# Double-norm roots in one power, dot products in two column parts, and tail weights sent earlier, in an eight-stage graph and feed-forward kernel

## What is computed

```
# layer 0, graph part: 8 heads, then a last attention with one head
h      = z @ W2                               # 128 x 768, summed over 8 heads (6144 rows of W2)
alpha_s, alpha_d = h @ a_src2, h @ a_dst2     # the two dot products
e      = leaky_relu(alpha_s[src] + alpha_d[dst]);  softmax over the edges of a node
out    = segment_sum(h[src] * alpha, dst)
# layer 2, feed-forward: a layer norm, and inside it a root-mean-square norm
y = (x - mean) / sqrt(var + 1e-5);  x_norm = y * rsqrt(mean(y*y) + 1e-6) * g;  quantise to integers
# layer 3, feed-forward: a layer norm, and inside it (router, attention) another one
n = (x - mean(x)) / sqrt(var(x) + 1e-5);  z = (n - mean(n)) / sqrt(var(n) + 1e-5)
```

## Time and profile before

| what | us |
|---|---|
| median of 3 runs | 380.73 (379.99 to 381.67) |
| time of the profiled execution | 379.25 |
| its span, from first to last instruction | 377.5 |
| outside the span | 1.75 |
| PE busy | 354.4 (94%) |
| DVE busy | 180.1 (48%) |
| ACT busy | 61.7 (16%) |
| POOL busy | 41.6 (11%) |

### The profile page before, as it was taken

One profiled execution on the slowest core, in us unless ns is written; L12 is line 12 of the kernel. 1 busy time (PEld: TensorE's weight loads), 2 busy tenths in 40 slices (PEclk: granted clock), 3 DMA queues, 4 the chain that ended last, 5 costly groups with the idle time before them and its releaser, 6 DMA issues.

```text
span 377.5 us, 4176 instructions
## 1 busy us (share of the span) xinstructions
PE 354.4 (94%) x1592; PEld 225.7 (60%) x1592; DVE 180.1 (48%) x541; ACT 61.7 (16%) x142; POOL 41.6 (11%) x70
## 2 busy tenths in 40 slices
PE   7999999899999999897899999982799999999997
PEld 3666665556575665464456556551365499967654
DVE  4926526584746554567627452436512401163341
ACT  2012010101120101021003210122000411064010
POOL 5900000010000002130130000402200200000000
PEclk9999999999999999999999999995599999999999
DMA  7999999897956171299999999834015700000001
GB/s 277 434 415 417 430 415 415 340 353 303 347 204 224 44 262 76 79 429 399 430 387 405 418 427 382 312 109 211 0 32 236 292 2 0 2 0 3 0 0 42
DMA packets 10453, 90.10 MB, mean 239 GB/s; under 512 B 2146, under 2 KB 2786, under 8 KB 6338
## 3 DMA queue, kind: packets, MB, share of 16 engines
q1 hardware_dynamic: 8238, 84.91, 56.3%
q0 software_dynamic: 800, 3.54, 2.6%
q10 hardware_dynamic: 1396, 1.40, 1.1%
HBM read 89.45 MB, written 0.39 MB: 238 GB/s over the span
## 4 chain that ended last, share of the span: by engine, by line
PE 86%; DVE 9%; issue 2%; POOL 1%; ACT 1%; DVEq 0%; POOLq 0%
PE ps L1448 14%; PE ps L1414 13%; PE ps L1392 8%; PE ps L1754 8%; PE ps L1330 4%; PE ps L1603 4%; PE ps L1622 4%; PE ps L1436 3%; PE ps L1477 2%; PE ps L1734 2%; PE ps L1830 2%; PE ps L1802 2%; PE ps L1850 2%; PE ps L1515 2%; PE ps L1350 2%
## 5 line engine op out<-in xcount | busy, mean ns | idle before, releaser
L1414 PE MATMUL ps<-ring,xT 128*128 128x512 f32 (+1 forms) x168 | 56.4, 486 | 0.0
L1448 PE MATMUL ps<-ring,h 128*128 128x512 f32 (+1 forms) x168 | 55.6, 486 | 0.0
L1448 PEld LDWEIGHTS ps<-ring,h 128*128 128x128 f32 x168 | 31.2, 190 | 21.9 <-issue 20.1
L1414 PEld LDWEIGHTS ps<-ring,xT 128*128 128x128 f32 x168 | 30.8, 191 | 19.5 <-issue 17.7
L1392 PE MATMUL ps<-ring,xT 128*128 128x512 f32 (+1 forms) x96 | 32.0, 487 | 0.1
L765 DVE CUSTOM_DVE_ANT_0 g<-h,avec 128x768 f32<-128x768 f32 x9 | 8.6, 959 | 36.7 <-ACT h L494 24.6
L372 POOL TENSOR_TENSOR rstd<-var,mhalf 128x1 f32<-128x1 f32 x10 | 6.4, 645 | 172.9 <-DVE var L707 86.9
L1392 PEld LDWEIGHTS ps<-ring,xT 128*128 128x128 f32 x96 | 17.8, 190 | 12.4 <-issue 11.3
L1330 PE MATMUL ps<-shiftm 128*128 128x512 bf16 x74 | 22.1, 455 | 2.1 <-POOL shiftm L390 2.1
L853 DVE TENSOR_SCALAR ring<-ring,idxb,ewb 128x128 bf16<-128x128 bf16 x99 | 22.5, 309 | 0.0
L494 ACT ACTIVATE h<-ps 128x768 f32<-128x768 f32 (+4 forms) x19 | 12.0, 644 | 58.9 <-PE ps L1414 16.2
(11 more groups left out here) (363 smaller groups left out, 480.9 us busy)
## 6 DMA issues: line engine op xcount, KB each, us to landing
ring<-in_gat_w SPq DMA_DIRECT2D x15, 2304.0 KB, 11.3
avec<-in_gat_a SPq DMA_DIRECT2D x9, 768.0 KB, 8.7
ring<-in_l_w SPq DMA_DIRECT2D x3, 2304.0 KB, 34.8
ring<-in_gat_w SPq DMA_DIRECT2D x6, 384.0 KB, 5.9
ring<-in_l_w SPq DMA_DIRECT2D x2, 1152.0 KB, 6.4
ring<-in_l1f_w1a SPq DMA_DIRECT2D x1, 2304.0 KB, 21.4
ring<-in_l1f_w1b SPq DMA_DIRECT2D x1, 2304.0 KB, 26.0
ring<-in_l1f_w2a SPq DMA_DIRECT2D x1, 2304.0 KB, 31.8
```

Source lines behind the costliest of these rows:

```text
L1414: last = mm(ps[:, at + lo:at + hi], xT[:, c, :], w[:, c, lo:hi], start=(c == 0), stop=(c == C - 1))
L1448: last = mm(ps[:, 4 * WIN + lo:4 * WIN + hi], h2[:, par * D + c * P:par * D + (c + 1) * P], w[:, c, lo:hi], start=False, stop=False)
```

## The change

Three things are edited. The double norms: POOL makes one power of a number that DVE has prepared, in place of a root and five more operations; in the last layer the single and the double root come out of one instruction over two columns, and DVE makes the once-normalised rows `xn` behind the scaling of the transposes in place of ahead of them. ACT's table load for Gelu stands ahead of the copy of the joined weights. The last attention: the dot products are made over columns 0 to 511 from `h1`, then over columns 512 to 767 from PSUM, and the two partial sums are added; the copy of the 256 columns comes behind them; and 7 of the edge matmuls move from ahead of the score row to behind it. The weights: `FIRST_SLOT` is 0, so units 0 to 3 go to slots 0 to 3, which the head stage frees one after the other, and unit 0 is issued ahead of the last `W2`.

```
 ]
-FIRST_SLOT = 4
+FIRST_SLOT = 0
 (U_L0, U_L1, U_L1W1A, U_L1W1B, U_L1W2A, U_L1W2B, U_L2, U_L3A, U_L3B, U_RIN, U_Q, U_RO1, U_K, U_V,
...
         rstd = sb("rstd", [P, 1])
-        mhalf = sb("mhalf", [P, 1])
+        mhalf2 = sb("mhalf2", [P, 2])
+        mhalf = mhalf2[:, 0:1]
         ones = sb("ones", [P, P])
...
             return cells[:, lo:lo + n]
-        again, twice = cell("again"), cell("twice")
+        twice, both_var, both_root = cell("twice"), cell("both_var", 2), cell("both_root", 2)
         fc1w = unit(U_RO1, "fc1", "p (c n) -> p c n", c=C)
...
             load_w2(6, 0)
+            sp.wait_ge(S["hprod"], 7)
+            load_unit(0)
             load_w2(7, 1)
             load_avec(8)
-            sp.wait_ge(s("edges_summed"), 1)
-            for u in range(len(UNITS)):
+            for u in range(1, len(UNITS)):
+                if u == 1:
+                    sp.wait_ge(S["hprod"], 8)
+                if u == 2:
+                    sp.wait_ge(S["w2_used"], 7)
+                if u == 3:
+                    sp.wait_ge(S["hprod"], 9)
                 if u == 4:
-                    sp.wait_ge(S["hprod"], 7)
-                if u == 5:
-                    sp.wait_ge(S["hprod"], 8)
-                if u == 6:
-                    sp.wait_ge(S["w2_used"], 7)
-                if u == 7:
-                    sp.wait_ge(S["hprod"], 9)
+                    sp.wait_ge(s("edges_summed"), 1)
                 if u >= SLOTS:
...
                 chained(pool, "pool_step", ins)
-            roots = [0]
-            def inverse_root(k):
-                roots[0] += 1
+            def inverse_root(k, root=rstd[:], of=var[:], half=mhalf):
                 pool.wait_ge(s("var_ready"), k)
-                pool.tensor_tensor(rstd[:], var[:], mhalf[:], ALU.pow).then_inc(s("rstd_ready"), 1)
-            def inverse_root_twice(k, eps):
-                inverse_root(k)
-                pool.wait_ge(s("rstd_ready"), roots[0])
-                link(pool.tensor_tensor(again[:, 0:1], rstd[:], rstd[:], ALU.mult))
-                link(pool.tensor_tensor(again[:, 0:1], again[:, 0:1], mv[:, 1:2], ALU.mult))
-                link(pool.tensor_scalar(again[:, 0:1], again[:, 0:1], eps, None, ALU.add))
-                link(pool.tensor_tensor(again[:, 0:1], again[:, 0:1], mhalf[:], ALU.pow))
-                pool.tensor_tensor(twice, again[:, 0:1], rstd[:], ALU.mult).then_inc(s("rstd_ready"), 1)
-                roots[0] += 1
-            link(pool.memset(mhalf[:], -0.5))
+                pool.tensor_tensor(root, of, half, ALU.pow).then_inc(s("rstd_ready"), 1)
+            link(pool.memset(mhalf2[:], -0.5))
             pool.memset(shiftm[:], 0.0).then_inc(S["pool_step"], 1)
...
             load_row(row1[:], "l3_b2")
-            inverse_root_twice(6, RMS_EPS)
+            inverse_root(6, twice)
             inverse_root(7)
...
             pool.dma_start(row0[0:MLP + 1, :], a["fc2"]).then_inc(s("in_fc2"), 16)
-            inverse_root_twice(9, LN_EPS)
+            inverse_root(10, both_root, both_var, mhalf2[:])
             load_row(avec[:, 0:D], "bo")
-            inverse_root(10)
+            inverse_root(11)
...
                 copy(join[:, lo:hi], ps[0:MLP + 1, 2 * WIN + lo:2 * WIN + hi]).then_inc(s("mlp_copied"), 1)
+            nc.scalar.activation(cell("scrap"), mhalf[:], ACT.Gelu)
             act.wait_ge(s("xb_ready"), 4)
             join_out(0)
-            nc.scalar.activation(cell("scrap"), mhalf[:], ACT.Gelu)
             affine_T("zhatT_ps", xT[:].rearrange("p c n -> p (c n)"), "r_ln", "xrT_ready")
...
             link(nc.vector.tensor_scalar(missing, missing, -1.0, 1.0, ALU.mult, ALU.add))
+            share = cell("alpha_share", 4)
+            dve.wait_ge(s("gat2_rows"), 1)
+            dve.wait_ge(S["avec_in"], 16 * 9)
+            dve.wait_ge(S["alpha_ready"], 8)
+            for k in range(2):
+                link(nc.vector.tensor_tensor_reduce(g3[:, 0:WIN], h1[:, 0:WIN], avec[:, k * D:k * D + WIN], 1.0, 0.0, ALU.mult,
+                                                    ALU.add, share[:, k:k + 1]))
             dve.wait_ge(S["hprod"], 9)
+            for k in range(2):
+                link(nc.vector.tensor_tensor_reduce(g3[:, WIN:D], bank(5, D - WIN), avec[:, k * D + WIN:(k + 1) * D], 1.0, 0.0,
+                                                    ALU.mult, ALU.add, share[:, 2 + k:3 + k]))
+            nc.vector.tensor_tensor(alpha[:, 0, :], share[:, 0:2], share[:, 2:4], ALU.add).then_inc(S["alpha_ready"], 1)
             nc.vector.tensor_copy(h1[:, WIN:D], bank(5, D - WIN)).then_inc(S["h_rows"], 1)
-            dve.wait_ge(s("gat2_rows"), 1)
-            head_alphas(8, 0)
+            wait(dve, "alpha_ready", 9)
             head_softmax(8, 0)
...
             link(nc.vector.bn_aggr(mv[:], stats[:].rearrange("p a b -> p (a b)")))
-            nc.vector.tensor_scalar(var[:], mv[:, 1:2], LN_EPS, None, ALU.add).then_inc(s("var_ready"), 1)
+            nc.vector.tensor_scalar(var[:], mv[:, 1:2], 1.0 + RMS_EPS, RMS_EPS * LN_EPS, ALU.mult, ALU.add) \
+                .then_inc(s("var_ready"), 1)
             dve.wait_ge(s("in_g_in"), 16)
...
             link(nc.vector.tensor_reduce(largest, g1[:], AX.X, ALU.max, apply_absolute_value=True))
-            dve.wait_ge(s("rstd_ready"), 7)
+            dve.wait_ge(s("rstd_ready"), 6)
             def integers(dst, tmp, root, n, parts):
...
             bits_y = h2[:, 0:BIT // 2].bitcast(BF16)
-            quantise(8, bits_y, y, row("g_out"), BIT, g1[:, 4 * BIT:5 * BIT])
+            quantise(7, bits_y, y, row("g_out"), BIT, g1[:, 4 * BIT:5 * BIT])
             worth_of(1, cell("unit_out"))
...
             add_residual(6, 0, x, cell("unit_out"))
-            normalise(9, xn, x, "xn_ready")
+            normalise(8, xn, x, "xn_ready")
             part_T(7)
...
-            whiten(10)
-            nc.vector.tensor_scalar(xn[:], x[:], mv[:, 0:1], rstd[:], ALU.subtract, ALU.mult).then_inc(S["dve_step"], 1)
-            used["dve_step"] += 1
-            dve.wait_ge(s("rstd_ready"), 11)
+            link(nc.vector.bn_aggr(mv[:], stats[:].rearrange("p a b -> p (a b)")))
+            nc.vector.tensor_scalar(both_var[:, 1:2], mv[:, 1:2], 1.0 + LN_EPS, LN_EPS * LN_EPS, ALU.mult, ALU.add) \
+                .then_inc(s("var_ready"), 1)
+            nc.vector.tensor_scalar(both_var[:, 0:1], mv[:, 1:2], LN_EPS, None, ALU.add).then_inc(s("var_ready"), 1)
+            dve.wait_ge(s("rstd_ready"), 9)
             for lo, hi in ((0, D // 2), (D // 2, D)):
-                nc.vector.tensor_scalar(g1[:, lo:hi], x[:, lo:hi], mv[:, 0:1], twice, ALU.subtract, ALU.mult) \
+                nc.vector.tensor_scalar(g1[:, lo:hi], x[:, lo:hi], mv[:, 0:1], both_root[:, 1:2], ALU.subtract, ALU.mult) \
                     .then_inc(s("zhat_ready"), 1)
...
             affine_T("zhatT_ps", g1, "ln1", "xaT_ready")
+            link(nc.vector.tensor_scalar(xn[:], x[:], mv[:, 0:1], both_root[:, 0:1], ALU.subtract, ALU.mult))
             def biased_T(dst, ps_at, bias):
...
             shift = cell("mean_share")
-            dve.wait_ge(s("rstd_ready"), 12)
+            dve.wait_ge(s("rstd_ready"), 10)
             link(nc.vector.tensor_scalar(shift, mv[:, 0:1], rstd[:], -1.0, ALU.mult, ALU.mult))
...
                 last.then_inc(s(signal), 1)
-            sum_edges(range(10, 25))
+            sum_edges(range(10, 18))
             score_row(8, 0)
-            sum_edges(range(25, EC)).then_inc(s("edges_summed"), 1)
+            sum_edges(range(18, EC)).then_inc(s("edges_summed"), 1)
             turn_attention(8)
```

## The result

The changed kernel took **376.68 us** (median of 5 runs, 376.11 to 377.56) against 380.54 for the kernel before (5 runs, 379.99 to 381.67) on the same chip. The ratio is 0.9899 with a 95% interval of 0.9875 to 0.9923, so it is faster by 3.86 us, about 1%. The time lies inside the predicted range, near its lower end, and 1.5 us under the forecast of 378.2. In a later set of 12 runs it took 377.38, ratio 0.9894 [0.9863, 0.9926]. Four of those 12 were in a slower state (about 381.8 us at a mean granted clock of 0.964; the other eight have a median of 376.66), and in this document a median is over all runs while a ratio leaves such executions out. The profiled execution took 376.11, of which 374.3 are span, against 379.25 and 377.5.

What follows compares the result with a forecast made beforehand. PE, busy 94% of the span, was taken to bound the kernel. Attention 1.25 and root-mean-square norm 1.30, with 0 for layer-norm and weights, came off the 380.73 median: 378.2 us, range 376.5 to 379.9.

Steps and rivals of the forecast that it cites:

- The last attention, 1.25 forecast: Last head's attention: split dot products and seven moved edge matmuls bring the turn to 156.85 from 158.12, taken as 1.25 us.
- The root-mean-square norm, 1.30 forecast: Root-mean-square double norm: DVE starts at 256.14, after its own reduction, in place of 257.44, a gain of 1.30 us.
- The layer-norm norm, 0 forecast: Last layer's double norm: PE is busy in L1734 until 296.89, so shorter POOL work wins 0.
- The weights, "earlier issue wins 0": Tail's weight units: all landed ahead of their use and no transfer stood in PE's waits, so earlier issue wins 0.
- DVE's copy was priced without its cover: Last attention: DVE's 0.42 us copy is covered by the score row's 0.53 us way to DVE; uncovered it would cost 0.42.
- The rival "the clock moves": Fillers behind the quantised feed-forward: clock rising earlier wins up to 1.6 us more (376.6, chance 0.12); rising at 272.5 gives 379.4.
- the 0.8 us around the sum that had a chance of 0.53: Whole kernel: the sum as worked out, a time within 0.8 us of 378.2, chance 0.53.
- A new wait that takes half: Last attention: slower PSUM dot products or DVE's copy delaying the softmax, 0.6 to 1.2 us less, 379.1; with clock, chance 0.23.
- The collision: SP's queue: unit 1 delays the last `W2`, PE stands 5.2 us ahead of L1515, 383.4, slower; chance 0.05.
- No effect: Whole kernel: PE's own work swallows both parts' gains, 380.7; no change to tell had chance 0.07.

Runs made afterwards that it cites:

- The experiment on both norms against one: Kernel before with only the root-mean-square norm's single power: 378.63 us, ratio 0.9935; with both norms' single powers and the earlier table load: 377.74 us, ratio 0.9930.
- the fillers: 24 more dummy PE matmuls in layer 2's quantised feed-forward: kernel before 378.37 us; changed kernel 376.64, and 376.87 in a second set.

## Why the prediction was right, and where it was off

*The last attention, 1.25 forecast: 1.33 measured.* Each term held (forecast in brackets): products in idle time 0.69 (0.69); from PSUM 0.42 (0.41); everything else up to the score row 0.30 (0.38); score row 153.86 (153.9); turn 156.79 (156.85). The addition of two columns took 0.16 and not 0.2. PE's next work and the softmax end together, 0.04 us apart (0.07), and undoing the move of the edge sums took 0.9 of it away. The Trainium skill ("VectorE: DVE Perf Modes", section "The TRN2 errata — SBUF-src ops pay a fixed extra latency per instruction") gives an fp32 addition as (N+151) cycles at 0.96 GHz, 0.42 us for 256 columns, and the dot product from PSUM took that; the same section's rule against small tiles did not decide, since the added parts lay in idle time.

*The root-mean-square norm, 1.30 forecast: 1.31 measured*, in every profile that has it. The reduction was late next.

*The layer-norm norm, 0 forecast: 0 measured.* The experiment on both norms against one shows it, and so does the last column of the table.

*The weights, "earlier issue wins 0": true alone, and too simple beside the attention's part.* This is the step that failed. I had read that no transfer stood among PE's waits, and didn't ask by how much unit 0 was early. I also read "6.4 us" as the landing of both its parts, where it is the median of two, 5.2 and 7.5. The second part before, and PE's first product with the unit:

```profile
157.44 0.43 SPq L320 DMA_DIRECT2D ring<-in_l_w  x1
```

```profile
ring<-in_l_w SPq DMA_DIRECT2D x1, 1152.0 KB, 7.5
```

```profile
165.81 0.81 PE L1548 MATMUL ps<-ring,xT 128*128 128x384 f32 x2
```

It landed at 157.44 + 7.5 = 164.9, 0.9 us early. My sum moved PE's need of it forward by 1.25 us and the issue, behind the last edge sum, came only 0.25 sooner, so by the rows of before it would have come just late: with the issue left there PE waited 0.23 and 0.95 us in two profiles, of which 0 and 0.84 reached the end of the stretch. DVE's copy was priced without its cover, and this transfer wasn't. The forecast of the whole didn't suffer, since the change has both parts.

*The clock.* The rival "the clock moves" named this mechanism and the fillers as the place: up to 1.6 more. The trace shows 1.03, and another 0.12 on the light matmuls. I had given it a chance of 0.12. With it the sum for the profiled execution is 376.7 - 1.15 = 375.55, and the 0.65 lost net around 170 us bring it to 376.2, where 376.11 was measured. The median came 1.5 us under the forecast: by the table this term, named but left out of the sum, is 0.8 to 1.2 of it, in every profile with the norm's edit, and so an effect of the change and not the luck of a run; that the range still covered it is due to the rival, not to the sum. So the time fell outside the 0.8 us around the sum that had a chance of 0.53, and where the rival with 0.12 had put it, at 376.6: the range and the sizes of both parts were right, and the sum lacked a term. That the low stretch in the ternary layer costs 2 us is shown by the fillers. Why the clock falls at 166 us in some executions, in the midst of busy matmuls, is not settled; it did so in other places too, between 175 and 187 and between 242 and 252, in kernels with and without the change, and no edit here was aimed at it. Whether the change makes such stretches rarer isn't shown either.

*The other rivals.* A new wait that takes half: not there, in the changed kernel; one came as soon as the weights were late, though not the one named. The collision: refuted by the order of landing. No effect: refuted by both traces.

## What to carry to other kernels

When PE's path gets shorter by x, list each transfer that PE needs within the next stretch and how early it lands; whatever is early by less than x becomes the new wait, even if it stands in no list of waits. An edit that wins nothing alone can be the cover of another, so test it with the other as well as without. Where the compared runs differ by about a per cent, cut several profiles at the same places of the busiest engine's list and compare stretch by stretch: each part's gain then stands out to some tenths of a microsecond, and what chance did lies in stretches that nobody edited. Don't compare executions of equal mean clock when the edit itself shortens a low stretch: the mean then hides a part of the gain.

## What the runs showed of the hardware

A dot product with its sum costs DVE as much as a plain addition of that width: 0.69 us for 512 columns of SBUF and 0.42 for 256 columns of PSUM, beside 0.68 and 0.41 for the additions of L888 with a PSUM operand, and 0.08 for the reading of the sum. In the changed kernel's profile POOL's power over one column took 0.55 to 0.66 us in eight places of L371 and 1.26 beside DVE's 768-column operation with two inputs in SBUF, where DVE's own took 1.01; over two columns, with DVE idle, it took 0.72. Two transfers of 2,304 KB issued behind each other on SP's queue landed in order of issue, 8.5 and 13.6 us after it, in whichever order they were issued (9.0 and 16.0 the other way, with 768 KB between them). The granted clock fell to the low level (0.50) in stretches in which PE had light matmuls and waits (255 to 272 us), and in some executions in stretches in which it was busy (166 to 169 us). With 24 more fillers in the first of these it stayed at 1.00 in the kernel before; in the changed kernel with the same fillers a low stretch came over the old fillers in both profiles (265.4 to 268.8 us in one).
